# The expert stage of a vision-tower layer in another order: first layer, mask and second layer of a quad one step behind its logits

## What is computed

```
h = attention(x)                      # 8x8 windows, 8 heads of 8, 2D RoPE, projection
h = h + selective_scan(layernorm(h))  # 16 states per channel, over the tokens of each image
h = h + experts(layernorm(h))         # argmax of 32 logits picks one expert per token
```

```
logits = xf @ router_w.T + router_b
idx = argmax(logits)
h = relu(xf @ W1[idx] + b1[idx])      # 64 -> 16
out = relu(h @ W2[idx] + b2[idx])     # 16 -> 64
```

## Time and profile before

| what | us |
|---|---|
| median of 3 runs | 681.51 (680.41 to 682.46) |
| the profiled execution's own time | 681.19 |
| span of its profile | 679.4 |
| expert stage in it | 449.5 to 679.4 |
| PE busy in the whole span | 575.5 (85%) |
| DVE, ACT, POOL busy | 490.1, 417.7, 307.4 |

### The profile page before, as it was taken

How to read it: one execution, slowest core, us unless ns; L and a number is a source line. 1 busy time by engine, 2 the same in 40 slices (tenths; PEclk the granted TensorE clock), 3 DMA queues, 4 the chain that set the end, 5 groups by cost and what they waited for, 6 DMA issues and landing times. The chain is left out here.

```text
span 679.4 us, 18439 instructions
## 1 busy us (share of the span) xinstructions
PE 575.5 (85%) x7207; PEld 388.3 (57%) x7208; DVE 490.1 (72%) x877; ACT 417.7 (61%) x723; POOL 307.4 (45%) x352
## 2 busy tenths in 40 slices
PE   3795489999999999999666667649999999999993
PEld 3321478888888888888422222235555555555551
DVE  3798377777777777777199899955667677676661
ACT  3597277778877788877489547504555545555451
POOL 5300235455554555543579569843233332333320
PEclk9899599999999999999787688878999999999997
DMA  9500222222222222220020000000101011011011
GB/s 193 92 1 8 62 53 51 51 58 54 52 56 48 57 55 53 52 52 18 1 28 0 1 0 0 3 2 1 25 19 24 20 22 24 18 24 23 18 26 23
DMA packets 62377, 23.29 MB, mean 34 GB/s; under 512 B 45778, under 2 KB 62162, under 8 KB 62290
## 3 DMA queue, kind: packets, MB, share of 16 engines
q1 hardware_dynamic: 61472, 21.96, 16.0%
q10 hardware_dynamic: 690, 0.13, 0.1%
q0 software_dynamic: 128, 0.00, 0.0%
HBM read 5.29 MB, written 4.19 MB: 14 GB/s over the span
## 5 line engine op out<-in xcount | busy, mean ns | idle before, releaser
L690 DVE TENSOR_REDUCE top<-psum 128x16 f32<-128x1024 f32 x64 | 78.0, 1219 | 61.5 <-PE psum L518 61.5
L627 ACT ACTIVATE prob_t<-psum 128x512 f32<-128x512 f32 x128 | 69.7, 595 | 27.9 <-PE psum L533 27.9
L533 PE MATMUL psum<-kc,prob 128*128 128x128 f32 x512 | 70.5, 282 | 11.9 <-ACT prob L619 8.9
L695 DVE TENSOR_TENSOR prob<-psum,top 128x1024 f32<-128x1024 f32 x64 | 78.4, 1225 | 2.2
L619 ACT ACTIVATE prob<-prob 128x1024 f32<-128x1024 f32 x64 | 67.7, 1059 | 15.2 <-DVE prob L695 15.2
L1640 ACT ACTIVATE hid<-psum,b1c 128x512 f32<-128x512 f32 x96 | 62.4, 691 | 17.8 <-PE psum L1548 17.8
L1556 PE MATMUL psum<-x_t,w1x 64*64 64x256 f32 x1024 | 71.8, 397 | 0.0
L484 POOL TENSOR_TENSOR rstd<-var,mhalf 128x4 f32<-128x4 f32 x32 | 32.2, 1008 | 86.0 <-DVE var L721 86.0
L533 PEld LDWEIGHTS psum<-kc,prob 128*128 128x128 f32 x512 | 56.3, 143 | 21.5 <-ACT prob L619 18.3
L1531 POOL TENSOR_TENSOR m_sq<-m_xc 128x256 f32<-128x256 f32 x32 | 19.6, 612 | 105.1 <-DVE m_xc L1695 105.0
L549 PEld LDWEIGHTS psum<-v_st,prob_t 128*64 128x64 f32 x2048 | 62.3, 138 | 6.2 <-ACT prob_t L627 6.0
(11 more groups left out here) (199 smaller groups left out, 1287.9 us busy)
## 6 DMA issues: line engine op xcount, KB each, us to landing
raw<-big_bc SPq DMA_DIRECT2D x256, 32.0 KB, 2.0
h_all<-in_x SPq DMA_DIRECT2D x16, 256.0 KB, 5.2
x_st<-big_a SPq DMA_DIRECT2D x32, 128.0 KB, 2.2
out<-out_st SPq DMA_DIRECT2D x128, 32.0 KB
kc<-constants SPq DMA_DIRECT2D x1, 458.0 KB, 4.2
w1x<-in_L_ffn_W SPq DMA_DIRECT2D x2, 128.0 KB, 4.2
w2x<-in_L_ffn_W SPq DMA_DIRECT2D x1, 128.0 KB, 3.9
wraw<-in_L_tok_qkv_w ACTq DMA_DIRECT2D x2, 32.0 KB, 4.7
```

Of the source, the lines that this page charges most:

```text
L533: m = pe.transpose(banks[4 + half][:, n * P:n * P + P], prob[:, f, at:at + 2, :], ident)
L627: act.activation(prob_t[:, f, 4 * half:4 * half + 4, :].rearrange("p j q -> p (j q)"), banks[4 + half][:, :], ACT.Copy).then_inc(prob_t_do ...
L690: dve.tensor_reduce(top[:, f, :].rearrange("p (g h) -> p g h", g=4), sc, AX.X, ALU.max).then_inc(top_done, 1)
L695: dve.tensor_tensor(prob[:, f].rearrange("p (g h) k -> p g h k", g=4), sc, top[:, f, :].rearrange("p (g h) -> p g h", g=4).unsqueeze(3).br ...
```

## The change

```diff
-        t["rwx"] = sb("rwx", [P, NE])
+        t["rwx"] = sb("rwx", [P, 2, NE])
...
-            pe.wait_ge(rw_read, 1)
+            pe.wait_ge(rw_read, 2)
...
             dve.memset(knee[:, :], KNEE).then_inc(knee_set, 1)
+            dve.memset(rwx[:, :, :], 0.0).then_inc(rwx_zeroed, 1)
...
-            dve.tensor_copy(rwx[:, :], psum[:, 7, 0:NE]).then_inc(rw_read, 1)
+            dve.wait_ge(rwx_zeroed, 1)
+            for b in range(2):
+                q = slice(64 * b, 64 * b + 64)
+                dve.tensor_copy(rwx[q, b, :], psum[q, 7, 0:NE]).then_inc(rw_read, 1)
...
-    x_t = sb("x_t", [P, 2, P])
+    x_t = sb("x_t", [P, 2, 2, P])
...
+    OUT_ORDER = (0, 2, 1, 3)
...
             def body(i):
+                if live(i, 0):
+                    pe.wait_ge(y_staged, i + 1)
+                    if not first(i):
+                        pe.wait_ge(h_done, i)
+                    if not first(i, 3):
+                        pe.wait_ge(out_made, i - 3)
+                    for n in range(2):
+                        m = pe.transpose(psum[:, 0, n * P:n * P + P], y_st[:, n, :], ident)
+                    m.then_inc(y_turned, 1)
                 if live(i, 2):
+                    pe.wait_ge(x_copied, i - 1)
+                    for g, b in X_PARTS[:4]:
+                        x_part(i - 2, g, b, True)
...
+                    pe.wait_ge(chosen, i - 1)
+                    if not first(i, 2):
+                        pe.wait_ge(mark_copied, i - 2)
+                    for s in range(4):
+                        if s == 3:
+
+                            pe.wait_ge(x_half, i * 16 - 24)
+                        m = pe.matmul(psum[0:96, 2, s % 2 * 256 + s // 2 * P:s % 2 * 256 + s // 2 * P + P],
...
+                    m.then_inc(mark_turned, 1)
+                if live(i, 3):
+                    pe.wait_ge(o_copied, i - 2)
+                    pe.wait_ge(h_done, min(i + 1, QUADS))
...
+                    m.then_inc(o_turned, 1)
+                if live(i, 1):
+
+                    pe.wait_ge(xh_done, i)
+                    if not first(i, 1):
+                        pe.wait_ge(lg_done, i - 1)
...
+                    m.then_inc(x_turned, 1)
+                if live(i, 2):
+                    for g, b in X_PARTS[4:]:
+                        x_part(i - 2, g, b, False)
                     if first(i, 2):
                         pe.wait_ge(masks_set, 2)
                     pe.wait_ge(mark_copied, i - 1)
                     for g in range(4):
                         mask(g)
...
                     pe.wait_ge(x_copied, i)
                     for k in range(2):
-                        for b in range(2):
-                            q = slice(64 * b, 64 * b + 64)
-                            m = pe.matmul(psum[:, LOGIT_BANK[b], 256 + k * NE:256 + k * NE + NE], x_t[q, k, :],
-                                          rwx[q, :], start=True, stop=True, skip_group_check=True)
-                            m.then_inc(logits_done, 1)
+                        m = pe.matmul(psum[:, 1, 256 + k * 2 * NE:256 + k * 2 * NE + 2 * NE], x_t[:, (i - 1) % 2, k, :],
+                                      rwx[:, :, :], start=True, stop=True, skip_group_check=True)
+                    m.then_inc(logits_done, 1)
...
-                    for g in range(4):
+                    for g in OUT_ORDER:
...
+            stage_y(0)
+
             def body(i):
...
+                if live(i, -1):
+                    act.wait_ge(y_turned, i + 1)
+                    stage_y(i + 1)
+                if live(i, 2):
+                    act.wait_ge(mark_turned, i - 1)
+                    act.activation(mark_t[:, :, :].rearrange("p b q -> p (b q)"), psum[0:96, 2, :], ACT.Copy
+                                   ).then_inc(mark_copied, 1)
+                if live(i, 1):
+                    act.wait_ge(x_turned, i)
...
+                if live(i, 3):
+                    dve.wait_ge(o_turned, i - 2)
+
+                    if not first(i, 3):
+                        dve.wait_ge(stored, i * 64 - 192)
+                    dve.scalar_tensor_tensor(out_st[:, :, :], psum[:, 0, 256:512].rearrange("p (s d) -> p s d", s=4),
...
+                if live(i, 0):
+                    dve.wait_ge(sq_done, i + 1)
+                    dve.tensor_reduce(ssum[:, :], sq[:, :, :], AX.X, ALU.add).then_inc(ssum_done, 1)
...
+                if live(i, 2):
+                    dve.wait_ge(hid_done, i * 4 - 5)
...
-                    dve.wait_ge(logits_done, i * 4)
...
+                    dve.wait_ge(logits_done, i)
```

More of the change, by code:

```diff
@@ L1550, in mask, with x_part @@
                           skip_group_check=True, tile_position=(32 * (g % 3), 0)).then_inc(hid_done, 1)
-            def x_part(g, b, start):
+            def x_part(i, g, b, start):
                 q = slice(64 * b, 64 * b + 64)
@@ L1557, in x_part @@
                                   w1x[q, g * 8 + 4 * c:g * 8 + 4 * c + 4, :],
-                                  x_t[q, :, :].rearrange("p k t -> p (k t)"), start=start, stop=False,
+                                  x_t[q, i % 2, :, :].rearrange("p k t -> p (k t)"), start=start, stop=False,
                                   skip_group_check=True)
@@ L1616, in body @@
                                 m.then_inc(o_done, 1)
[L1617 to L1632, removed]
             steps(pe, body)
@@ L1641, in relu, with stage_y @@
                                ).then_inc(relu_act, 1)
+            def stage_y(i):
+                act.activation(y_st[:, :, :].rearrange("p k (r x) -> p k r x", r=8),
+                               raster(y, i // 2 * 512 + i % 2 * 32), ACT.Copy).then_inc(y_staged, 1)
+            stage_y(0)
             def body(i):
[L1644 to L1649, removed]
+                if live(i, -1):
[7 more added lines that the diff above has]
+                    act.wait_ge(x_turned, i)
+                    act.activation(x_t[:, (i - 1) % 2, :, :].rearrange("p k t -> p (k t)"), psum[:, 1, 0:256], ACT.Copy
+                                   ).then_inc(x_copied, 1)
                 if live(i, 2):
@@ L1654, in body @@
                     relu(i, 0)
-                if live(i, 1):
-                    act.wait_ge(x_turned, i)
-                    act.activation(x_t[:, :, :].rearrange("p k t -> p (k t)"), psum[:, 1, 0:256], ACT.Copy
-                                   ).then_inc(x_copied, 1)
-                if live(i, 2):
                     relu(i, 1)
@@ L1666, in body @@
                                    ).then_inc(o_copied, 1)
-                if live(i, 1):
-                    act.wait_ge(mark_turned, i)
-                    act.activation(mark_t[:, :, :], psum[0:96, 1:3, 0:256], ACT.Copy).then_inc(mark_copied, 1)
             steps(act, body)
@@ L1675, in body @@
             def body(i):
-                if live(i, 2):
-                    dve.wait_ge(hid_done, i * 4 - 5)
-                    if not first(i, 2):
-                        dve.wait_ge(o_done, i * 2 - 4)
-                    dve.tensor_scalar(hid[:, 2, :], psum[:, HID_BANK[2], :], b1c[:, 2:3], 0.0, ALU.add, ALU.max
-                                      ).then_inc(relu_dve, 1)
                 if live(i, 0):
@@ L1708, in body @@
                                       ALU.is_equal).then_inc(eq_done, 1)
-                if live(i, 0):
-                    dve.wait_ge(sq_done, i + 1)
-                    dve.tensor_reduce(ssum[:, :], sq[:, :, :], AX.X, ALU.add).then_inc(ssum_done, 1)
-                if live(i, 1):
                     dve.wait_ge(eq_done, i)
@@ L1716, in body @@
                                       ).then_inc(rank_done, 1)
-                if live(i, 0):
-                    dve.wait_ge(ssum_done, i + 1)
-                    dve.tensor_scalar(var[:, :], ssum[:, :], 1.0 / C, LN_EPS, ALU.mult, ALU.add
-                                      ).then_inc(var_done, 1)
-                if live(i, 1):
                     dve.wait_ge(rank_done, i)
@@ L1730, in body @@
                                       ).then_inc(chosen, 1)
-                if live(i, 3):
-                    dve.wait_ge(o_turned, i - 2)
-                    if not first(i, 3):
-                        dve.wait_ge(stored, i * 64 - 192)
-                    dve.scalar_tensor_tensor(out_st[:, :, :], psum[:, 0, 256:512].rearrange("p (s d) -> p s d", s=4),
-                                             0.0, h_all[:, bass.ds(i * 4 - 12, 4), :], ALU.max, ALU.add
-                                             ).then_inc(out_made, 1)
             steps(dve, body)
```

46 lines of the change are left out of this document (20 added, 26 removed).

## The result

The changed kernel took 670.75 us (median of 4, 668.66 to 673.12) against 681.01 (median of 4). The ratio of the two is 0.9845, with a 95% interval of 0.9819 to 0.987: faster by 1.5%, where 2.1% were forecast, and 3.75 us above the forecast of 667.0. That is inside the stated range, which reaches to 674 because it takes in most of rival A. The profiled execution took 670.87 us, its span is 669.1.

The account below looks back on a forecast made before the run. PE was taken to set the pace, with about 0.3 us of waits a step. Savings of 9.0 (steady step), 0.7 (start), 0.8 (steps 32, 33) and 4.1 (end) cut the span from 679.4 to 664.8; forecast 667.0 us, range 663 to 674.

Parts of the forecast that it names:

- rival A: Second layer: relu exposed further, ACT 0.3 late or tile-shape changes costing more; step about 6.40, 672.7 us; chance 0.20.
- the 0.76 that it takes off: Steps 32 and 33: two pairs of y and one of x transposes that they don't have, 0.76 us less.
- The steady step: PE from mask to mask in the expert stage: 6.21 us, 0.30 less than 6.51; bounds 6.11 and 6.36.
- y transposes 0.27: PE between second layer and layer one: 0.22 to 0.27 us, no wait, as y was staged a step ahead.
- at most 0.44: Logits on PE with block-diagonal weights: four records take at most 0.44 us where the old eight took 0.56.
- the text's own signs: Steady step: logits to second bias below 0.44; wrong if masks are above 6.4 apart or second layer takes over 1.9.
- The waits of before: Old step on PE: about 0.3 us are waits, ahead of the logits for x_t and in layer one for the mark.
- The uncovered relu: Mask to second layer on PE: the chain mask, relu 0 on ACT, second layer is bare, 1.22 us; bounds 1.22 and 1.24.
- Order 0, 2, 1, 3: Second layer's groups on PE: this order just fits the ends of the relus, so no group waits and it takes 1.82.
- Everything said to be hidden: Steady step: mark, add, variance, output, mark_t and x_t come in time; DVE has 0.57 us to spare before relu 2.
- First steps: Start of the expert stage: second mask moves from 469.57 to 468.87, 0.7 us less; bounds 0 and 1.5.
- C: Ring DVE, POOL, DVE becomes the bound if POOL's power and product hold DVE off: ring 7.15, 695 us; chance 0.07.

Follow-up runs that it names:

- the variance late: Kernel before, with DVE's reduction and variance of a quad moved behind the choice of the quad before, in place of between its operations; 688.07 us.
- two edits that each eased one part of the old step: Each alone in the kernel before: x_t copy ahead of relu 0 on ACT, 678.09 us; DVE's reduction and variance behind the choice, 688.07 us.
- the kernel with five changes of shape: Changed kernel regrouped: layer one in one row, all transposes in another, relu ahead of variance and choice, second layer 0, 1, 2, 3; 673.52 us, ratio 0.9881.

## Why the prediction was right, and where it was off

- **Direction and ends: right.** The last mask to the last output was to be 4.62 and is 4.57, and outputs 30 and 31 are 5.49 apart (5.50). The two-buffer run shows that the stores were the bound. The last two steps take 11.87 together, 11.66 in the forecast (the 0.76 that it takes off is 0.81 by its own terms).
- **The steady step: right in sign, off in size.** The sum gave 6.21, the trace 6.41. The failing terms are "y transposes 0.27" (0.37), "x 0.27" (0.31), "o 0.22" (0.25), logits "at most 0.44" (0.59, which makes mask to second layer 1.25 in place of 1.22), and "second layer 1.82" (1.85); 0.10 + 0.04 + 0.03 + 0.03 + 0.03, less 0.03 in layer one and the mark, are the 0.20. To the last mask that is 5.9 us. By two of the text's own signs this part was wrong: masks above 6.4 apart, and logits not below 0.44; 6.41 also lies above its bound of 6.36. For y, x and part of the logits the cause is one: an interval was carried over to a place with other neighbours. The 0.27 had been read ahead of a group of the same shape. Ahead of layer one the x transposes take 0.31, and the y transposes, with another shape in front as well, 0.37. What made the o transposes and the second layer 0.03 longer is not shown.
- **The waits of before were overstated, and misread.** The text took the y transposes' 0.47 against a twin of 0.22 or 0.27 and called about 0.3 of the step waits. The twin stood ahead of its own shape; ahead of another, two transposes take 0.31 to 0.37 by themselves, so that the wait for `x_t` came to 0.10 to 0.16. The wait for the mark was 0.09, but it covered a change of shape: with no wait there, the mark's transposes take 0.42 in place of 0.35 (569.73 to 570.15 with the variance late). So PE's own work in the old step was 0.53 + 0.27 + 0.22 + (0.31 to 0.37) + 0.57 + 0.13 + 1.83 + 1.03 + 0.42 + 1.03 = 6.34 to 6.40, an estimate from those intervals that was not measured by itself. The new order took 0.1 to 0.2 us of waits out of the step and left PE with 6.41 of its own.
- **The uncovered relu: right.** Mask to second layer without logits is 1.22. The block-diagonal weights bring nothing, as forecast, though for a weaker reason: they are no shorter at all (0.59 against 0.56). On the length of the full-height logits the rule of the Trainium skill (TensorE: Matmul & The Clock Gate, "LDWEIGHTS (loading the stationary operand)" and "The mechanism"), 0.66 as an estimate, came nearer than my bound; behind another full-height group they take 0.49. The total by that rule, 3 to 4 us above 667.0, is where the measurement came out, but not for its reason: without the logits the step is still 6.41.
- **Order 0, 2, 1, 3: right**, worth 0.15 a step here.
- **Everything said to be hidden was hidden.** PE has no wait left in the steady step. DVE idles 0.64 us ahead of relu 2 (0.57 forecast):

```profile
551.15 0.75 DVE L1718 TENSOR_SCALAR hid<-psum,b1c 128x512 f32<-128x512 f32 x1 [0.64 <-PE psum L1553]
```

- **First steps: better than forecast, and not for its reason.** The second mask came at 467.28, not 468.87; 0.91 of that is a stage that began earlier. From the first y copy to the second mask it took 18.72 us, where the kernel before took 20.10 and the forecast had 19.40. The forecast gave 0.7 to the y transposes that no longer wait for `xh`; no run shows that term. The two runs with the y transposes between mask and logits and the one without logits have the new order too and took 19.87 to 20.09, as the old one does. What differs is the granted clock, which in the changed kernel was 1.00 from 459 us on; in the kernel before the same view has 0.50 still at 461 to 463 us:

```profile
461.00:463.00 2.00, 2.00 (x20) 0.62 (x12) 0.00 (x0) 0.54 (x2) 0.00 (x0) 0.50 0.00 0
```

 This hid part of the error, which was luck: the steps were forecast 5.9 us too short, the second mask 1.6 too late, and the span came out 4.3 above its forecast.
- Of the rivals, A came nearer than the forecast itself: its step was 6.40, and its 672.7 is 1.95 off where 667.0 is 3.75 off. It had two conditions. The one in its title, that ACT is late, did not come (the three relus take 1.84 together in the run without logits, where the text had 3 x 0.67); the other, that changes of tile shape cost more in the new neighbourhoods, did, and the text gave it no price of its own. C did not come in the steady step: POOL's power runs beside relu 2, and its product, from 545.26 to 545.87, ends before the choice's first operation with two SBUF inputs (546.11). But the contention is real, and the trace of before had not shown it (last section).

## What to carry to other kernels

When a group of matmuls is moved, cost it with the shapes of its new neighbours: on this kernel two more changes of PE's tile shape cost 0.31 us and one less saved 0.21, with nothing waiting, so 0.16 to 0.21 each, nearly as much as a short group itself (0.22). Order PE's groups so that equal shapes stand together, and put them where the engine would otherwise wait for another one's result. And before a wait is counted as gain, look for the other rings of the same length: two edits that each eased one part of the old step left it at 6.52 or made it 6.70, and it took the same interval in three kernels to see that DVE's way to the mark held it.

## What the runs showed of the hardware that was not expected

The start of the expert stage isn't the same from run to run. The granted clock of PE is 0.50 there until some point, and that point moves by several us whatever the kernel is. The kernel with two output buffers, in stretches of time:

```profile
455.00:459.00 4.00, 3.22 (x30) 1.85 (x32) 2.87 (x10) 0.17 (x1) 2.24 (x3) 0.50 0.01 2
463.00:466.00 3.00, 3.00 (x20) 2.09 (x22) 2.82 (x12) 0.87 (x2) 0.99 (x2) 0.50 0.00 0
466.00:468.00 2.00, 2.00 (x12) 0.78 (x12) 0.38 (x1) 0.33 (x1) 1.25 (x2) 0.50 0.00 0
```

PE was busy for all of 463 to 466 us at the 1.2 GHz level and went on so until 468; its first two masks are 9.64 us apart. In the changed kernel they are 6.39 apart, at 1.00 from 459 us. The variant with the y transposes moved had 6.62 and 6.20 in its two profiles, and 9.08 with the other order of groups. The stage itself began between 446.2 and 450.6 us over fourteen profiles of twelve kernels that are alike up to there but for the router weights.

The time from the first y copy to the second mask follows the moment at which the clock reaches 1.00, in the old order and the new:

| clock at 1.00, behind the first y copy | first y copy to second mask | profiles |
|---|---|---|
| 10.4 to 11.0 us | 18.6 to 18.8 (19.3 with two more shapes) | 5 of the new order |
| 13.7 to 14.8 us | 19.9 to 20.1 | 3 of the old order, 3 of the new |
| 19.9 to 20.8 us | 22.7 to 22.9 | 2 of the old order, 1 of the new |

Whether the new order brings the early moment more often isn't shown by so few. So some 4 us of a single run's time say nothing about the change, and the steady step, the same to 0.01 us in both kernels that were profiled twice (but for single steps up to 0.05 longer), is the better witness.

The second surprise is the contention that the prediction had set aside. In the first steps of the changed kernel POOL's product meets a comparison or a product of DVE, both sides with two operands in SBUF:

```profile
457.38 0.72 POOL L1543 TENSOR_TENSOR m_xh<-m_xc,m_rstd 128x256 f32<-128x256 f32 x1
457.67 0.58 DVE L1731 TENSOR_TENSOR rank<-rank,kc 128x128 f32<-128x128 f32 x1
462.93 0.61 POOL L1543 TENSOR_TENSOR m_xh<-m_xc,m_rstd 128x256 f32<-128x256 f32 x1
462.97 0.72 DVE L1728 TENSOR_TENSOR rank<-lg,best 128x128 f32<-128x128 f32 x1
```

The DVE rows take 0.58 and 0.72 us where they take 0.29 alone; the second ends 0.15 us after the product does. A mark beside POOL's power had kept its 0.56. In the kernel with five changes of shape the mark starts beside the product in the steady step, and there it takes 0.67 (566.86, product until 567.12). So on these rows it is the product, which reads 256 elements of a partition, that holds DVE, and not the power, which reads 4. The Trainium skill (GPSIMD Engine Reference, "Specifications") has this contention for VectorE instructions with two SBUF inputs; these rows agree with it, and the row of the power did not. In the steady step of the changed kernel the two miss each other by a quarter of a us, which is chance, not design: in its repetition one step met the product (0.71 at 576.00), without a longer step.
